# All 32 images emitted one behind the other on every engine, in place of a loop over pairs of images

## The reference

```python
x = x + conv3x3(sign(batchnorm(group_norm(x))), sign(W) * mean|W|)   # binarized convolution
t = tokens(x)                                                       # 32 x 3136 x 32
# linear attention, 16 heads of 32, elu(.)+1 on q and k, cos/sin position weights
kv  = sum_s k_cos v + sum_s k_sin v;  o = (q_cos kv_cos + q_sin kv_sin) / (q . sum k + 1e-5)
t = t + o @ dense_w.T + dense_b                                     # input: layer norm of t
# mixture of 8 experts, the best 2 by router softmax
t = t + sum_k p_k * (layernorm(t) @ expert_w[k] + expert_b[k])
```

## Time and profile before

| | us |
|---|---|
| median of 3 runs | 2601.42 |
| lowest and highest run | 2597.09, 2603.22 |
| the profiled execution, whole | 2608.5 |
| its span, first to last instruction | 2606.6 |
| busy PE / DVE / POOL / ACT | 2302.2 / 2190.3 / 1733.6 / 1559.9 |
[...]

### The profile page before, as it was taken

How to read it: one execution, slowest core, us unless ns; L and a number is a source line. 1 busy time by engine, 2 the same in 40 slices (tenths; PEclk the granted TensorE clock), 3 DMA queues, 4 the chain that set the end, 5 groups by cost and what they waited for, 6 DMA issues and landing times.

```text
span 2606.6 us, 51821 instructions
## 1 busy us (share of the span) xinstructions
PE 2302.2 (88%) x15908; PEld 1110.7 (43%) x15908; DVE 2190.3 (84%) x2976; ACT 1559.9 (60%) x2757; POOL 1733.6 (67%) x1415
## 2 busy tenths in 40 slices
PE   3458999999999999999999999999999999999962
PEld 3313444444444434444443444444443444444431
DVE  3447899899898989899898989889898989999962
ACT  0046766567666666576666666666666657666620
POOL 0123477777776777777677767767676777777675
PEclk7579999999999999999999999999999999999985
DMA  8211112122221211122211111222111122211001
GB/s 249 49 28 24 33 33 38 32 42 42 42 42 33 34 31 35 36 42 41 42 34 30 34 33 39 42 42 42 31 35 31 34 38 42 41 35 32 20 19 25
DMA packets 284893, 105.84 MB, mean 41 GB/s; under 512 B 246032, under 2 KB 279680, under 8 KB 284512
## 3 DMA queue, kind: packets, MB, share of 16 engines
q1 hardware_dynamic: 284640, 102.41, 19.9%
HBM read 31.19 MB, written 12.85 MB: 17 GB/s over the span
## 4 chain that ended last, share of the span: by engine, by line
PE 57%; DVE 21%; issue 11%; POOL 3%; ACT 3%; DMA 2%; SPq 2%; DVEq 0%; ACTq 0%; POOLq 0%
PE ps L576 11%; PE ps L627 9%; PE ps L567 6%; PE ps L601 6%; DVE qbuf L981 6%; PE ps L618 5%; PE ps L592 4%; DVE kbuf L975 4%; PE ps L652 3%; DVE rs L998 2%; PE ps L553 2%; PE ps L646 2%; PE ps L560 2%; PE ps L640 2%; DMA qbuf<-in_x 2%
## 5 line engine op out<-in xcount | busy, mean ns | idle before, releaser
L701 ACT ACTIVATE ebuf<-ps,small 112x1024 f32<-112x1024 f32 x448 | 499.4, 1115 | 357.4 <-PE ps L567 306.4
L795 POOL TENSOR_TENSOR qbuf<-spread_r,qbuf 128x896 f32<-128x896 f32 x224 | 468.6, 2092 | 354.5 <-ACT spread_r L736 354.5
L975 DVE SCALAR_TENSOR_TENSOR kbuf<-ps,ebuf 112x1024 f32<-112x1024 f32 x448 | 544.3, 1215 | 106.6 <-ACT ebuf L701 103.0
L706 ACT ACTIVATE ebuf<-ps,small 128x896 f32<-128x896 f32 x448 | 451.8, 1009 | 206.4 <-PE ps L592 150.5
L981 DVE SCALAR_TENSOR_TENSOR qbuf<-ps,ebuf 128x896 f32<-128x896 f32 x448 | 485.5, 1084 | 15.8 <-ACT ebuf L706 14.6
L576 PE MATMUL ps<-kbuf,xcs 112*64 112x512 f32 x1792 | 482.9, 617 | 6.8 <-DVE kbuf L975 6.2
L627 PE MATMUL ps<-qbuf,gmat 128*64 128x224 f32 x3584 | 387.2, 358 | 2.9 <-DVE pbuf L1009 2.9
L778 POOL TENSOR_TENSOR rstd<-varr,power 112x28 f32<-112x28 f32 x64 | 307.3, 4802 | 80.9 <-DVE varr L960 77.4
L567 PE MATMUL ps<-wk,z 128*112 128x512 f16 x896 | 287.7, 404 | 61.0 <-DVE qbuf L981 33.6
L824 POOL TENSOR_TENSOR prod<-prod 112x512 f32<-112x512 f32 x224 | 285.5, 1275 | 54.7 <-DVE prod L1065 54.7
L627 PEld LDWEIGHTS ps<-qbuf,gmat 128*64 128x64 f32 x3584 | 240.2, 136 | 155.7 <-issue 81.9
(11 more groups left out here) (131 smaller groups left out, 3090.7 us busy)
## 6 DMA issues: line engine op xcount, KB each, us to landing
z<-zhl SPq DMA_DIRECT2D x1024, 49.0 KB, 1.9
qbuf<-in_x SPq DMA_DIRECT2D x8, 1568.0 KB, 12.2
xt<-in_x SPq DMA_DIRECT2D x256, 49.0 KB
out<-ffn SPq DMA_DIRECT2D x256, 49.0 KB
shifted<-nat SPq DMA_DIRECT2D x128, 52.6 KB, 5.1
qbuf<-in_sel SPq DMA_DIRECT2D x1, 1024.0 KB, 12.0
tabn<-in_tabnc SPq DMA_DIRECT2D x1, 784.0 KB, 14.1
p<-in_p2c SPq DMA_DIRECT2D x1, 528.0 KB, 10.5
```

The lines of the kernel that those rows point to most:

```text
L701: act.activation(ebuf[0:PT, 0, :].rearrange("p (a b) -> p a b", a=2), o[0:PT, :, :], ACT.Exp, bias=minus_one[0:PT, :]).then_inc(kexp_made, 1)
L706: act.activation(ebuf[:, 1, 0:2 * G * PT].rearrange("p (a b) -> p a b", a=2), o[:, :, 0:G * PT], ACT.Exp, bias=minus_one).then_inc(qexp_ma ...
L795: nc.gpsimd.tensor_tensor(qbuf[:, 2:4, n, :], spread_r[:, :, :], qbuf[:, 2:4, n, :], ALU.mult)\
L975: v.scalar_tensor_tensor(kbuf[:, n % 2, :].rearrange("p (a b) -> p a b", a=2), o[0:PT, :, :], 1.0, ebuf[0:PT, 0, :].rearrange("p (a b) -> ...
```

## The change

The loop goes. `walk` emits all 38 iterations as straight code on all five engines, in the order that they had. The number of steps, their order, tiles, buffers and semaphores stay; what were register values become constants, and the code that derived them is dropped.

```diff
-LOOP_FIRST, LOOP_LAST = 3, B - 4
@@ lookup
-        if t is not None:
-            (_, no2, before2), last = table[kind, m + 2, n], LOOP_LAST - LOOP_FIRST - 1
-            slot_z, no_z, before_z = table[kind, m + last, n]
-            assert no_z == no + (no2 - no) * (last // 2) and slot_z == slot
-            assert before_z == (before[0], before[1] + last, before[2])
-            no = t * (no2 - no) + no
@@ walk
     for i in ITERATIONS:
-        if i < LOOP_FIRST:
-            run(i)
-    with eng.Fori(0, (LOOP_LAST + 1 - LOOP_FIRST) // 2) as t:
-        run(LOOP_FIRST, t)
-        run(LOOP_FIRST + 1, t)
-    for i in ITERATIONS:
-        if i > LOOP_LAST:
-            run(i)
+        run(i)
```

## The result

The changed kernel takes 2529.64 us in the median of 4 runs (2525.98 to 2532.11) against 2600.06 for the kernel before (4 runs, 2597.09 to 2603.22); the ratio is 0.9728, with a 95% interval of 0.9711 to 0.9745. The profiled execution took 2532.1 us around a span of 2530.3; its mean granted clock was 0.960, against 0.954 in the kernel before. In the spans that is 76.3 us less, in the medians 70.4. One execution of the kernel in which DVE alone loops took 4385.5 us against 2532.4 to 2533.4 of its three others, and nothing is concluded from it.

What follows compares the result with a forecast made beforehand. PE was taken to bound plain images, with branches back lengthening every second one. Branches gave 69.3 us, registers and fetch 0: 2601.4 - 69.3 = 2532.1 us, range 2521 to 2547, chance 84%.

Steps and rivals of the forecast that it cites:

- Branches back: Loop over images: removing 12 taken branches per engine saves the long images' excess, 69.3 us, 5.8 per branch.
- The split that I gave of one branch: Per branch: some 3.65 us PE stop, up to 1.8 from ACT's, plus matmuls at a lowered clock, 1.9 and 3.4 us.
- Register instructions: Values computed in the loop become constants: gain between 0 and 6.0 us, taken as 0.
- the 71.3 to 71.5 that I had named: Sign: ktsb copies on ACT follow each other at 71.3 to 71.5 us from image 328 to 2326, without alternation.
- The doubt I named: Unprofiled runs, 7.1 us faster, may have fewer lowered clocks at branches: only 62.2 us to give back, result 2539.2 us.
- Instruction fetch: Straight text is fetched once in order, hidden behind PE's matmuls: cost 0 to 6.0 us, taken as 0.
- Fewer packets, no more: Instruction packets over the span, 166 on q8 and 87 on q14 before, were expected to fall, not rise.
- (a): Rival: images lengthen when nothing stops PE; 24 images growing 1 us each give 2556 us; chance 8%.
- (b): Rival: the stop comes with something else every two images and stays; only branch instructions go, 2601 us; chance 3%.
- (c): Rival: fetch of straight text doesn't keep up with PE; at 0.84 us per packet 2671 us; chance 2%.

Runs made afterwards that it cites:

- the near branches: Changed kernel with an empty two-trip loop on PE behind iterations 4, 6, ... 26, so 12 taken branches to targets some instructions back; 2530.7 us.
- DVE with a long body: Changed kernel with only DVE looping, over a body of six images with 4 trips, the other engines straight; 2538.2 us in one run.
- the announced loop: Changed kernel with all five engines looping 13 trips over two images, as in the kernel before, each branch back announced by `hint_back_edge`; 2552.7 us.

## Why the prediction was right, and where it was off

The forecast of 2532 us was within 3 us. The mechanism of its one large term, the branches, held in every run that tested it; that the point came so close is partly luck, since two smaller errors nearly cancelled.

**Branches back.** 69.3 us were set for the long images. Cut in the same way, the 23 images that took 1712.21 us would take 23 x 71.20 = 1637.6 us at the new period, 74.6 less, of which 23 x 0.23 = 5.3 us are the shorter plain image and 69.3 the branches. The split that I gave of one branch was right in kind but not in size: PE's 3.65 us are not all on the path: in a plain image PE has 71.20 - 68.83 = 2.4 us of idle time, and the stop costs less than its own length, so I take it that part of it takes the place of that time. A stop costs 2.4 us of period, the lowered clock 1.9 and ACT's stop 1.0. As the clock fell behind 10 of the 12 stops, that makes 2.4 + 1.6 + 1.0 = 5.0 us of the mean 5.8; the rest shows only when all engines stop, and its cause is open.

**Register instructions.** This term failed: "I take 0, since PE's busy time falls by 0.07 to 0.22 us in the same rows, which explains most of it". The plain image went from 71.43 to 71.20 us, 0.23 x 26 = 6.0 us, the far end of my bound. The lower busy time of PE in the earlier trace rows was no sign of missing work; in the changed kernel the images from 470 to 2179 us have 68.8 to 68.9 us with the same 490 matmuls. By the legend of the page the ends of matmuls are modelled, so a difference of 0.2 us in PE's busy time can't serve as a control for work. The copies came at 71.2 us and not at the 71.3 to 71.5 that I had named. The runs put the 0.23 us on ACT (0.19) and DVE (0.08); which of their computed values delay PE, and on what way, no run shows.

**From the profile to the median.** The medians differ by 70.4 us where the spans differ by 76.3. The doubt I named fits that: the other runs would have had less to give back at the branches than 69.3 us, about 70.4 - 6.0 = 64.4, close to the 62.2 of that reading. The record supports it in part. In the 24 executions of the kernel before that were made beside the experiments, the time goes with the mean granted clock: the four fastest (2594.5 to 2596.7 us) had 0.957, the four slowest (2608.5 to 2615.8) 0.949 to 0.951. A straight line through them has 2604 us at the 0.9535 of the profiled execution, so by this estimate the clock accounts for about half of the 8.4 us that it lay above 2600.06. The two errors, -6.0 and about +5 us, nearly cancelled; the point is better than its terms.

**Instruction fetch.** The packets on q8 fell from 166 to 130, three for each of the 12 branches of PE (with PE alone in a loop they are 166 again, and q14 stays at 92), and no gap appeared. "Fewer packets, no more" was wrong for q14, which rose from 87 to 92. It has 70 with DVE alone in a loop and 127 with ACT alone, so part of the bodies had been fetched once and not in each trip, DVE's among them.

**The rivals.** (a), longer images without rest: 24 images at 71.20 us, and the granted clock stays at 1.00 from 470 to 2179 us. (b), no change: refuted by the result and by the near branches. PE's near branches took 0.21 us, its far ones 3.65 us in the median, and the records of the other four engines 40 to 67 ns, so the stop isn't that of every branch. A stop that waits for the fetch of the target agrees with the near and far branches of PE, the announced ones, DVE's two bodies, and the one q8 packet within each far branch; how far a target must lie for it, no run here shows. (c), a slow fetch of straight text: nothing of it seen.

## What to carry to other kernels

Price a hardware loop by the difference of two periods, one with a branch back and one without, and do so for each engine: the record of the branch (45 ns on ACT) can be far from its cost (1.0 us of period). Some branches back were free here: PE's to a near target (2530.7 us against 2529.6 without), and DVE's over a body of two images (71.26 us with a branch, 71.30 without). The others that were measured, without an announcement, stopped their engine for 1.6 to 1.8 us (ACT), 2.6 (DVE with a long body) or 3.3 to 3.9 (PE) per trip, and on PE 10 of the 12 stops of the kernel before also had a granted clock of 0.50 behind them. So unroll first the loop of the engine that bounds the kernel (52 of 70 us), and announce the branch where the loop must stay (47 of 70 us). Loops may differ from engine to engine, which also makes the cheapest experiments.

## What the runs showed of the hardware that I had not expected

- A stop on PE of 3.3 to 3.9 us lowered the granted clock in most cases, not in all: 10 of 12 in the kernel before and in the one where PE alone loops. None of the 12 stops of 1.4 to 1.9 us in the announced loop did. The length alone doesn't decide it: with PE alone in a loop the clock fell behind a branch of 3.52 us and did not fall behind one of 3.59 us.
- DVE's branch back is free with a body of two images, though ACT's is not. The counts on the page (2976 against 2757) mislead here, since the sequencers' instructions are not in them: in the trace one trip has 381 instructions on DVE and 394 on ACT with them. Which bodies are fetched again in each trip isn't settled by these runs.
- Computed values cost 0.19 us per image on ACT (71.39 against 71.20 us), 0.08 on DVE (71.28) and nothing on PE (71.17).
